# Edge stage of a graph network: results scattered four groups late from four places, rows gathered in pairs while the pipeline fills, and a second order of steps for the first turns

## The reference

```python
h = concat([x[senders], x[receivers]], -1)       # gathers, 2 x 256
h = tanh(h @ W0 + b0)                            # 512 -> 406
h = tanh(h @ W1 + b1)                            # 406 -> 323
h = h @ W2 + b2                                  # 323 -> 256
h = h * (e_embed @ Wg)                           # edge features 128 -> 256
out = segment_sum(h, senders) / max(count, 1)
```

## Time and profile before

| | us |
|---|---|
| runs | 3194.13 median of 3 (3191.09 to 3195.50) |
| profiled execution | 3194.94 |
| its span, first to last instruction | 3193.2 |
| PE, PEld busy | 3072.1 (96%), 2497.9 (78%) |
| DVE, ACT, POOL busy | 2243.9 (70%), 1566.8 (49%), 1395.7 (44%) |
| mean granted TensorE clock | 0.989 of full |

### The profile page before, as it was taken

One profiled execution on the slowest core, in us unless ns is written; L12 is line 12 of the kernel. 1 busy time (PEld: TensorE's weight loads), 2 busy tenths in 40 slices (PEclk: granted clock), 3 DMA queues, 4 the chain that ended last, 5 costly groups with the idle time before them and its releaser, 6 DMA issues. The chain is left out here.

```text
span 3193.2 us, 65358 instructions
## 1 busy us (share of the span) xinstructions
PE 3072.1 (96%) x17339; PEld 2497.9 (78%) x17340; DVE 2243.9 (70%) x5602; ACT 1566.8 (49%) x3155; POOL 1395.7 (44%) x1485
## 2 busy tenths in 40 slices
PE   7699999999999999999998989999999999999899
PEld 6588888888888888888886767777777888887666
DVE  7688888888888888888886989995655222245522
ACT  2366666666666666666663777771111111011354
POOL 3577777777777777777763222220000000000111
PEclk9899999999999999999998999999999999999999
DMA  5555555555555555555554888887566777778475
GB/s 167 167 164 161 163 164 164 164 164 160 164 164 164 163 163 164 164 164 163 163 152 134 261 253 264 265 264 224 170 182 195 225 220 224 219 233 262 88 120 95
DMA packets 298299, 584.82 MB, mean 183 GB/s; under 512 B 43361, under 2 KB 150842, under 8 KB 298234
## 3 DMA queue, kind: packets, MB, share of 16 engines
q1 hardware_dynamic: 180960, 280.20, 29.7%
q0 software_dynamic: 90416, 254.46, 28.6%
q10 hardware_dynamic: 26858, 49.32, 4.2%
HBM read 493.97 MB, written 110.32 MB: 189 GB/s over the span
## 5 line engine op out<-in xcount | busy, mean ns | idle before, releaser
L976 PE MATMUL bank<-parts,ring 128*128 128x512 f32 x2500 | 623.3, 398 | 5.5 <-DVE T_buf L1748 2.4
L976 PEld LDWEIGHTS bank<-parts,ring 128*128 128x128 f32 x2500 | 460.9, 188 | 106.7 <-issue 6.6
L621 POOL DMA_INDIRECT msgs<-rows_out,sidx x416 | 408.2, 981 | 152.1 <-issue 95.4
L614 POOL DMA_INDIRECT p_in<-p_tab,gidx x416 | 403.6, 970 | 138.7 <-issue 114.9
L614 POOL DMA_INDIRECT q_in<-q_tab,gidx x416 | 398.1, 957 | 126.8 <-issue 125.6
L676 PE MATMUL bank<-hidden1h,w1h 128*108 128x512 f32 x936 | 406.7, 434 | 3.2 <-DVE hidden2l L864 3.2
L676 PE MATMUL bank<-w2h,hidden2h 108*128 108x256 f32 x1248 | 402.4, 322 | 0.0
L677 PE MATMUL bank<-hidden1l,w1h 128*108 128x512 f32 x936 | 368.6, 394 | 0.0
L678 PE MATMUL bank<-hidden1h,w1l 128*108 128x512 f32 x936 | 367.4, 393 | 0.0
L1132 PE MATMUL bank<-at_dst,at_src 128*128 128x320 f32 x1088 | 327.1, 382 | 36.8 <-DVE at_src L1092 29.4
L783 ACT ACTIVATE hidden2h<-bank,b1c 108x512 fp32r<-108x512 f32 (+1 forms) x312 | 214.9, 689 | 296.7 <-PE bank L692 296.7
(11 more groups left out here) (252 smaller groups left out, 6056.4 us busy)
## 6 DMA issues: line engine op xcount, KB each, us to landing
ring<-counts SPq DMA_DIRECT2D x500, 320.0 KB, 3.3
R_buf<-msgs SPq DMA_DIRECT2D x544, 130.0 KB, 3.1
counts<-cells ACTq DMA_DIRECT2D x125, 320.0 KB, 3.3
eT<-in_edge_T SPq DMA_DIRECT2D x104, 256.0 KB, 2.9
R_buf<-counts POOLq DMA_DIRECT2D x25, 480.0 KB, 5.2
R_buf<-counts POOLq DMA_DIRECT2D x25, 320.0 KB, 5.6
p_in<-p_tab,gidx POOLq DMA_INDIRECT x416, 3.2
q_in<-q_tab,gidx POOLq DMA_INDIRECT x416, 3.2
```

The lines of the kernel that those rows point to most:

```text
L614: pool.indirect_dma_start(out=rows_in[:, z, c], out_offset=None, in_=tab[:], in_offset=bass.IndirectOffsetOnAxis(ap=gidx[:, z, which, c:c ...
L621: pool.indirect_dma_start(out=msgs[:], in_=rows_out[:, z, c], in_offset=None, out_offset=bass.IndirectOffsetOnAxis(ap=sidx[:, z, c:c + 1], ...
L976: mm = pe.matmul(bU[t].rearrange("p (w c) -> p w c", w=2), ring[:, cell(odd, a), t * P:(t + 1) * P].bitcast(dt), parts[k % 2][:, :, a].bit ...
```

## The change

It does four things. Results get four places (OUTS) instead of two, one semaphore for each place instead of one for each place and chunk, and a scatter runs four groups behind the W1 product instead of two. The loop has four turns in a round instead of two. In POOL's turns -3 to -1 the gathers go in pairs, p and q of one chunk, then the next. And PE, ACT and DVE get orders of their own for the first turns: `first_turn` (turn 0), `first_turns` (DVE, turns -2 to 0) and `early_turn` (turns 1 and 2), in which the steps of the older group come first.

```diff
 EXACT = 256
 OB = 16
+OUTS = 4
@@ -546,8 +547,8 @@
             gate = R_buf[:, 2 * GC * H1T * P:][:, 0:GC * D].rearrange("p (c n) -> p c n", c=GC)
             gidx = esb("gidx", [P, 2, 2, GC], I32)
             eT = esb("eT", [P, 2, GC * C])
-            rows_out = esb("rows_out", [P, 2, GC, RW])
-            sidx = esb("sidx", [P, 2, GC], I32)
+            rows_out = esb("rows_out", [P, OUTS, GC, RW])
+            sidx = esb("sidx", [P, OUTS, GC], I32)
             in_bucket = esb("in_bucket", [P, 2, GC, BK], BF16)
             in_p = esb("in_p", [P, 2, GC, P], BF16)
             in_a = esb("in_a", [P, 2, GC, T], BF16)
@@ -555,7 +556,7 @@
             place = esb("place", [P, GC])
 
             s_in_rows = [[esem(f"s_in_rows{z}{c}") for c in range(GC)] for z in range(2)]
-            s_sc = [[esem(f"s_sc{z}{c}") for c in range(GC)] for z in range(2)]
+            s_sc = [esem(f"s_sc{o}") for o in range(OUTS)]
             s_eT = [esem(f"s_eT{z}") for z in range(2)]
             s_idx, s_add, s_T, s_th1, s_lo1 = (esem(n) for n in ("s_idx", "s_add", "s_T", "s_th1", "s_lo1"))
             s_L1, s_th2, s_lo2, s_L2, s_gt, s_msg = (esem(n) for n in ("s_L1", "s_th2", "s_lo2", "s_L2", "s_gt", "s_msg"))
@@ -572,24 +573,38 @@
                     self.it, self.a = it, a
 
                 def group(self, k):
-                    return 2 * self.it + (self.a + k)
+                    return OUTS * self.it + (self.a + k)
 
                 def slot(self, k):
                     return (self.a + k) % 2
 
                 def use(self, k):
-                    return self.it + (self.a + k) // 2
+                    return OUTS // 2 * self.it + (self.a + k) // 2
+
+                def out(self, k):
+                    return (self.a + k) % OUTS
+
+                def out_use(self, k):
+                    return self.it + (self.a + k) // OUTS
 
                 def has(self, k):
                     return not isinstance(self.it, int) or 0 <= self.group(k) < G
 
+            def filling(t):
+
+                return isinstance(t.it, int) and t.group(0) < 0
+
+            def early(t):
+
+                return isinstance(t.it, int) and 0 < t.group(0) < 3
+
             def edge_loop(eng, body, first, head, tail, last):
 
                 for i in range(first, head):
                     body(Turn(0, i))
-                assert (tail - head) % 2 == 0
-                with eng.Fori(0, (tail - head) // 2) as it:
-                    for u in range(2):
+                assert (tail - head) % OUTS == 0
+                with eng.Fori(0, (tail - head) // OUTS) as it:
+                    for u in range(OUTS):
                         body(Turn(it, head + u))
                 for i in range(tail, last):
                     body(Turn(0, i))
@@ -617,14 +634,14 @@
 
                 def scatter(t, c):
 
-                    z = t.slot(-2)
-                    pool.indirect_dma_start(out=msgs[:], in_=rows_out[:, z, c], in_offset=None,
-                                            out_offset=bass.IndirectOffsetOnAxis(ap=sidx[:, z, c:c + 1], axis=0)
-                                            ).then_inc(s_sc[z][c], 16)
+                    o = t.out(-LAG)
+                    pool.indirect_dma_start(out=msgs[:], in_=rows_out[:, o, c], in_offset=None,
+                                            out_offset=bass.IndirectOffsetOnAxis(ap=sidx[:, o, c:c + 1], axis=0)
+                                            ).then_inc(s_sc[o], 16)
 
                 def body(t):
 
-                    if t.has(-2) and t.has(1):
+                    if t.has(-2) and t.has(3):
                         pool.wait_ge(s_L2, t.group(-2) * GC + 3)
                     if t.has(3):
                         pool.wait_ge(s_idx, t.group(3) + 1)
@@ -632,30 +649,31 @@
                         stand_alone(pool, s_up)
                         for c in range(GC):
                             gather(t, c, p_tab, 0, p_in)
-                    if t.has(0):
+                            if filling(t):
+                                gather(t, c, q_tab, 1, q_in)
+                    if t.has(0) and t.has(3):
                         pool.wait_ge(s_L1, H2T * t.group(0) + 1)
                         stand_alone(pool, s_up)
-                    if t.has(3):
+                    if t.has(3) and not filling(t):
                         for c in range(GC):
                             gather(t, c, q_tab, 1, q_in)
-                    ending = isinstance(t.it, int) and t.group(0) >= G
-                    if t.has(-2):
-                        pool.wait_ge(s_place, t.group(-2) + 1)
+                    ending = isinstance(t.it, int) and t.group(-LAG) >= G - 2
+                    if t.has(-LAG):
+                        pool.wait_ge(s_place, t.group(-LAG) + 1)
                         if not ending:
-                            if t.has(-1):
+                            if t.has(3):
                                 pool.wait_ge(s_L2, t.group(-1) * GC + 1)
-                            pool.wait_ge(s_msg, (t.group(-2) + 1) * GC)
+                            pool.wait_ge(s_msg, (t.group(-LAG) + 1) * GC)
                             stand_alone(pool, s_up)
                         for c in range(GC):
                             if ending:
-                                pool.wait_ge(s_msg, t.group(-2) * GC + c + 1)
+                                pool.wait_ge(s_msg, t.group(-LAG) * GC + c + 1)
                                 stand_alone(pool, s_up)
                             scatter(t, c)
 
-                edge_loop(pool, body, -3, 4, G - 4, G + 2)
-                for z in range(2):
-                    for c in range(GC):
-                        pool.wait_ge(s_sc[z][c], 16 * (G // 2))
+                edge_loop(pool, body, -3, LAG, G - 4, G + LAG)
+                for o in range(OUTS):
+                    pool.wait_ge(s_sc[o], 16 * GC * (G // OUTS))
 
             @blk.tensor
             def _(pe):
@@ -735,7 +753,32 @@
                     pe.wait_ge(s_took, j + 1)
                     add_to_ranks(t, rest_b, isinstance(j, int) and j == G - 1).then_inc(s_next, 1)
 
+                def first_turn(t):
+                    for m in range(H2T):
+                        first(t, m)
+                        transposes(t, m)
+                    transposes(t, H2T)
+
+                def early_turn(t):
+                    second(t, 0)
+                    places_before(t)
+                    second(t, 1)
+                    first(t, 0)
+                    transposes(t, 0)
+                    second(t, 2)
+                    first(t, 1)
+                    transposes(t, 1)
+                    second(t, 3)
+                    transposes(t, 2)
+                    first(t, 2)
+                    transposes(t, 3)
+                    places_after(t)
+
                 def body(t):
+                    if isinstance(t.it, int) and t.group(0) == 0:
+                        return first_turn(t)
+                    if early(t):
+                        return early_turn(t)
                     transposes(t, 0)
                     transposes(t, 1)
                     first(t, 0)
@@ -794,7 +837,30 @@
                     wait(act, s_msg, (j - 1) * GC + c + 1)
                     act.copy(gate[:, c], bO[c % 2][:, D:2 * D]).then_inc(s_gt, 1)
 
+                def first_turn(t):
+                    for m in range(H2T):
+                        second_tanh(t, m)
+                        first_tanh(t, m)
+                    first_tanh(t, H2T)
+
+                def early_turn(t):
+                    gate_out(t, 0)
+                    gate_out(t, 1)
+                    second_tanh(t, 0)
+                    first_tanh(t, 0)
+                    gate_out(t, 2)
+                    second_tanh(t, 1)
+                    first_tanh(t, 1)
+                    gate_out(t, 3)
+                    first_tanh(t, 2)
+                    second_tanh(t, 2)
+                    first_tanh(t, 3)
+
                 def body(t):
+                    if isinstance(t.it, int) and t.group(0) == 0:
+                        return first_turn(t)
+                    if early(t):
+                        return early_turn(t)
                     first_tanh(t, 0)
                     first_tanh(t, 1)
                     second_tanh(t, 0)
@@ -889,10 +955,10 @@
                     v.wait_ge(s_took, j + 1)
                     ch.start(j)
                     ch.link(v.tensor_reduce(place[:], ranked[:], mybir.AxisListType.X, ALU.add))
-                    for c in range(GC):
-                        wait(v, s_sc[z][c], 16 * t.use(-1))
-                    v.tensor_copy(sidx[:, z], place[:])
-                    v.tensor_copy(rows_out[:, z, :, D:RW], meta[:, bass.ds(j * GC, GC), :]).then_inc(s_place, 1)
+                    o = t.out(-1)
+                    wait(v, s_sc[o], 16 * GC * t.out_use(-1))
+                    v.tensor_copy(sidx[:, o], place[:])
```

(56 more changed lines are left out.)

3 lines of the change are left out of this document (2 added, 1 removed).

## The result

| | before | changed |
|---|---|---|
| median of 6 runs | 3193.3 us (3191.09 to 3197.11) | 3210.74 us (3205.67 to 3214.12) |
| ratio, 95% interval | | 1.0054 (1.0043 to 1.0065) |
| profiled execution, its span | 3194.94, 3193.2 | 3214.12, 3212.2 |
| ends of turns 1, 3, 51, 101, 104 | 155.00, 185.50, 918.16, 1681.74, 1716.91 | 145.58, 182.96, 913.55, 1692.29, 1727.48 |

The kernel became slower by 17.4 us of the median. I had forecast 3191.5 and no measurable difference; the range ended at 3197.5. The two profiled executions differ by 19.2: of the changed kernel's six it is the slowest, 3.4 above their median.

A forecast was written before the change was run, and what follows sets the result against it. PE was taken to bound the edge stage, with GpSimd full as well. 3194.9 (profiled) - 0.6 (fill) - 2.0 (stalls) = 3192.3; the profiled execution lies 0.8 above the median, so 3191.5 expected, range 3184.5 to 3197.5.

The forecast's parts named there:

- needs 15.19 us for a turn's 12: GpSimd in the edge stage: 1.266 us per transfer, 15.19 us for a turn's 12, so full as well as PE.
- scatters four groups behind: GpSimd skips two groups of scatters, some 10 us, while filling and repays them at the end; counted as nothing.
- some ten us: GpSimd's lead between a gather and its add in steady turns, taken as the cover for its pace.
- Rival 4: GpSimd becomes the bound in the loop, the stalls' 2.0 not gained: 3194 to 3197; chance 0.03, plus 0.02 for slower.
- The stalls: DVE's 0.3 us stall in the loop falls from 48 times to 23; 25 fewer at 0.08 gain 2.0 us.
- The fill: First turns: 8.0 us gained at turn 1, some 0.6 left at the end of turn 3.
- Both forecast waits: PE waits 2.7 us at turn 2's first W2 product and 3.2 us at turn 3's first transposes.
- The low clock I booked for turn 3: One stretch of PE at the 1.2 GHz level in turn 3, costing 1.57 us.
- The one for turn 1: One stretch of PE at the 1.2 GHz level in turn 1, 1.57 us, ending that turn at 147.0.
- rival 1: The fill's gain of 8.0 us at turn 1 stays: 3184.1; more than 4.4 us kept has chance 0.20.
- rival 3: PE's round of some 770 instructions is not held; 25 backward branches stall 1.0 us each: 3216.5; chance 0.04.
- The end: End of the stage: GpSimd's idle stretches take the extra scatters, the last scatter waits for the last message; nothing counted.

The follow-up runs named there:

- e13: The kernel before with the four waits for a place's scatters moved ahead of the product of ranks; 3221.01 us, ratio 1.0089.
- e10: The kernel before with one semaphore for each place's scatters instead of four; 3219.87 us.
- e16: The kernel before with the change's first turns and gathers in pairs alone, on a chip like the first; 3194.49 us, ratio 1.0000.
- e9: The changed kernel with each DVE add of gathered rows in the loop writing two columns instead of all; 3195.08 us.
- e1: The changed kernel with scatters two groups behind, as before, instead of four; 3197.7 us, ratio 1.0012.
- e3: The changed kernel with DVE's add of the second chunk ahead of the low part of the third; 3212.59 us, ratio 1.0062.
- e12: Same kernel as e16 (the kernel before with the change's first turns alone), on the chip with slower q gathers; 3221.18 us, one run 3190.28.
- the second four kernels: Four follow-up kernels on a chip that held PE's clock at 0.91 to 0.97 in the edge stage; the kernel before took 3678 us there.

## Why the prediction was wrong, point by point

**The step that failed** is the reading that GpSimd "needs 15.19 us for a turn's 12" transfers, and the one that rests on it, "scatters four groups behind: I count nothing". The 1.266 us is the window's 300 us over 237 transfers, and 237 counts one that began before the window; the 236 that began in it give 1.271. (The working written there, 228.07 over 237 and 0.30 more, gives 1.262 and 15.15, which is too low as well.) From start to start over 96 transfers the kernel before mostly needs 1.271 to 1.273, which is 15.26 to 15.28 a turn. PE's mean turn before was 15.27. I had both numbers within reach and did not see that they are one: the two engines ran level. PE's 15.22 without the stalls is below what GpSimd can do, so what I booked as a gain of 2.0 started a race that GpSimd loses by 0.04 a turn, and by 0.13 with its collisions. The cover of "some ten us" between a gather and its add was not the one that counted: from the end of the first q gather to its add it is 13.3 us at group 10 of the changed kernel and still 7.0 when DVE waits in every turn. The scatters' was, with 7.3 us of which 1.5 are the landing.

**Rival 4** was the right mechanism with a chance of 0.05 and a wrong price. I charged it with "nor more than 3 lost". A held turn, one in which GpSimd is the bound, costs not the difference of the two engines (0.05) but 0.35 over PE's 15.22, since a held GpSimd meets DVE's add in every turn (54 slow gathers in 50 turns). Against the 15.27 of before that is 0.30, and over 50 turns 15.2. What would have shown it: the trace of before has the collision as well, in three gathers above 1.1 us.

**The stalls**: the price of one was right (0.08 forecast, 2.1 over the 24 that are gone up to turn 51 is 0.09). The number was not: all vanish, since the one left in four is 0.14 and PE does not feel it, where I kept 23 of 48. That 2.1 by turn 51 looks like my 2.0 for the whole loop is luck.

**The fill** was the best part. I had counted from the stage's start in the trace of before; the changed execution's stage began 1.77 sooner. With 1.77 added the first add is at 108.7 (108.7 forecast), the first W1 tile at 119.4 (119.2), and turns 1, 2 and 3 end at 147.4, 165.1 and 184.7 (147.0, 164.9 and 184.9); from the first gather to turn 3 it gained 0.8 for a forecast of 0.6. Both forecast waits are there:

```profile
148.34 0.36 PE L694 MATMUL bank<-w2h,hidden2h 108*128 108x256 f32 x1 [2.29 <-issue]
```

```profile
164.52 0.66 PE L688 MATMUL bank<-ident,R_buf 128*128 128x128 f32 x4 [0.74 <-DVE hidden1h L918]
...
166.89 0.63 PE L688 MATMUL bank<-ident,R_buf 128*128 128x128 f32 x4 [1.71 <-DVE hidden1h L918]
```

2.29 stands for my 2.7, and 0.74 + 1.71 for my 3.2. The low clock I booked for turn 3 is there too (granted clock 0.50 from 168 to 171 us). The one for turn 1 is not (1.00 from 130 to 163), and that turn 1 ends right all the same is luck: the W2 product began 1.8 later than I walked it (130.60, or 132.4 by the start of before, for 130.6). From the first gather to the end of turn 3 the change takes 81.7 us, before 82.5; e13 and e10, with the old first turns, take 81.3 and 80.9. Of the gain at turn 1, 7.6 us from the first gather, 0.8 is left at turn 3, so rival 1 falls; and in e16 the early turns are worth nothing that its 12 runs can tell (0.9991 to 1.0009).

**The long loop** (rival 3): no gap. All turns of a round of about 770 instructions are 15.22 while PE leads, and in the changed kernel's trace the two instruction queues (q8, q14) move no packet between 249 and 1650 us. The Trainium skill (Runtime: NRT & Kernel Launch, Instruction fetch mechanics) has two statements, a larger memory for PE and two lines of 256 instructions; the trace agrees with the larger memory for PE and not with the two lines, by which each round would stall.

**The end**: "nothing again" was wrong by 4.0, the DRAIN. No row of before could price it, but the change of semaphores deserved a line in the sum.

**The sum** that the runs support: 0 for the fill, -2.1 (turns 4 to 51), +15.2 (52 to 101), +4.0 (DRAIN): +17.1, measured +17.4. The turns and the DRAIN are read from one execution of each kernel, so that the two agree to 0.3 is in part luck.

## What to carry to other kernels

When two engines are both full, a stall on one may be what keeps the other from being overtaken: compare their periods start to start over a hundred operations before removing it. Giving the slower one relief first is the step that follows from this; only e9, which leaves out sums, comes near it. A lead that is used up is seen in the slack between a transfer and its user at the start, middle and end of a long loop, not in busy shares. A collision that is rare while two engines drift becomes permanent when one waits for the other, so price the state in which one waits, not the drift.

## What the runs showed of the hardware

- **A gather is held up by an add of two SBUF operands.** In the traces of before, the change, e1, e3 and e13, 225 of the 227 gathers that began 0.1 to 0.3 us behind the start of a 128x384 add took over 1.1 us, and all 261 gathers above 1.1 began within 0.4 of one. The later it starts behind the add the less it loses: 1.23 us at 0.1 to 0.2, 1.15 at 0.2 to 0.3, 1.01 at 0.3 to 0.4 and 0.96 beyond, but for 1.03 at 0.5 to 0.6, where the add's second part (128x128) has just begun. The Trainium skill (SBUF, State Buffer, Who interferes with whom) states that a DVE instruction with two SBUF inputs contends with a GpSimd instruction that reads SBUF; the trace agrees, if the gather reads its indices there. Scatters seldom lie there; where they do, they grow too (up to 1.18 in e1, 1.33 in e3).
- **It works the other way too.** In the kernel before, where an add's second part starts together with a transfer of GpSimd (within 0.05 us), the add can be the one that grows: the mean of 55 such is 0.31 against 0.29 for the others, and the longest are 0.35:

```profile
515.01 0.29 DVE L834 TENSOR_TENSOR R_buf<-p_in,q_in 128x128 f32<-128x128 f32 x1
```

```profile
1186.93 0.32 DVE L834 TENSOR_TENSOR R_buf<-p_in,q_in 128x128 f32<-128x128 f32 x1
```

```profile
1186.93 0.95 POOL L614 DMA_INDIRECT q_in<-q_tab,gidx  x1 [0.30 <-issue]
```

  From 851 us on (turn 48) this is so in about every second turn, and the odd turns there have grown from 15.29 to 15.30 to 15.36. I read it as a contact that keeps the two level; it was not tried by itself, and it is not the whole of it.
- **Two engines that run level were held there.** In the kernel before, GpSimd's lead (the table above) stays between 6.0 and 6.4 from group 10 to group 38, falls within a few turns, and stays between 4.7 and 5.1 from group 43 to group 97. DVE waits for no gather or scatter there. Two paces that differ by chance would drift apart, so something couples them; what does so up to turn 38 is open.
- **DRAIN** on GpSimd at a block's end: 3.25 us with a semaphore per chunk, 7.25 to 8.4 with shared ones (six and twelve traces). Why is open.
- **Two outcomes of one program.** On the chip where GpSimd's q gathers took 0.3% longer, the kernel before ran at 3189 to 3198 or 3217 to 3225. The second group is as long as e12's, whose trace shows GpSimd overtaken at turn 28; no trace of such a run of before was taken, so that GpSimd was overtaken in it is not shown. The record gives this chip the same number as the one of the second four kernels; whether the chip or its condition made the difference is open.
